# A selective scan inside a decoder: row-tiled 0/1 broadcasts of B and C, the gate's sigmoid on ScalarE, the gated output behind the first scan, and twelve inverse roots moved to the attention before

## What is computed

```python
z = h @ in_w.T                         # h: (16, 128, 256) after an RMS norm, z: 64 channels
gate = jax.nn.silu(h @ gate_w.T)
A = -jnp.exp(A_log)                    # 64 channels x 16 states
Bi, Ci = z @ Bp_w.T, z @ Cp_w.T        # 16 states for each row
dt = jax.nn.softplus(z @ dt_w.T + dt_b)
A_bar = 1.0 + dt[..., None] * A
state = a_bar * state + dtz_t[:, :, None] * b_t[:, None, :]    # one step in time
y = jnp.sum(state * c_t[:, None, :], axis=-1)
out = (y * gate) @ out_w.T
```

## Time and profile before

| | |
|---|---|
| median of three runs | 2480.36 us (2477.17 to 2481.49) |
| the profiled execution's own time | 2478.89 us |
| its span | 2477.2 us |
| PE busy | 2197.7 us (89%) |
| DVE busy | 1678.8 us (68%) |
| ACT busy | 1319.8 us (53%) |
| POOL busy | 808.0 us (33%) |

### The profile page before, as it was taken

How to read it: one execution, slowest core, us unless ns; L and a number is a source line. 1 busy time by engine, 2 the same in 40 slices (tenths; PEclk the granted TensorE clock), 3 DMA queues, 4 the chain that set the end, 5 groups by cost and what they waited for, 6 DMA issues and landing times. The chain is left out here.

```text
span 2477.2 us, 49397 instructions
## 1 busy us (share of the span) xinstructions
PE 2197.7 (89%) x17742; PEld 1801.8 (73%) x17744; DVE 1678.8 (68%) x3260; ACT 1319.8 (53%) x3083; POOL 808.0 (33%) x1022
## 2 busy tenths in 40 slices
PE   6979799999698797989999989999689897999774
PEld 5857587888476696778888568888568686888652
DVE  4767644774676596764677647666578785888858
ACT  4558635665487563542666343333487464545345
POOL 5656502333255442100233202222210100454365
PEclk9999979999899899979999999999799999999888
DMA  3000082113400000051211430000200003777710
GB/s 114 2 1 2 1 340 84 52 52 125 154 2 2 22 2 1 2 203 70 105 52 51 173 118 1 1 2 1 103 1 1 1 1 96 226 212 217 223 29 34
DMA packets 102936, 178.41 MB, mean 72 GB/s; under 512 B 59687, under 2 KB 71591, under 8 KB 97578
## 3 DMA queue, kind: packets, MB, share of 16 engines
q1 hardware_dynamic: 85514, 135.93, 16.5%
q0 software_dynamic: 9792, 28.85, 3.6%
q10 hardware_dynamic: 7392, 10.49, 1.2%
HBM read 112.44 MB, written 62.78 MB: 71 GB/s over the span
## 5 line engine op out<-in xcount | busy, mean ns | idle before, releaser
L2365 POOL TENSOR_TENSOR l2a_Pn<-l2a_Pn,l2a_rden 128x1024 f32<-128x1024 f32 x32 | 60.0, 1897 | 284.1 <-DVE l2a_rden L2604 284.1
L1631 ACT ACTIVATE l0f_w_parts<-l0f_W 128x512 fp32r (+1 forms) x117 | 90.4, 775 | 64.8 <-PE l0f_psG L1436 50.4
L1789 DVE TENSOR_TENSOR l0f_w_parts<-l0f_W,l0f_w_parts 128x512 fp32r<-128x512 f32 (+1 forms) x117 | 99.3, 867 | 37.5 <-ACT l0f_w_parts L1631 37.4
L1631 ACT ACTIVATE l1f_w_parts<-l1f_W 128x512 fp32r (+1 forms) x117 | 90.6, 775 | 62.9 <-PE l1f_psG L1436 50.2
L4197 POOL TENSOR_TENSOR l3x_Pn<-l3x_Pn,l3x_fac 128x616 f32<-128x616 f32 (+2 forms) x96 | 70.4, 761 | 150.4 <-DVE l3x_fac L4276 140.6
L1789 DVE TENSOR_TENSOR l1f_w_parts<-l1f_W,l1f_w_parts 128x512 fp32r<-128x512 f32 (+1 forms) x117 | 99.4, 867 | 12.4 <-ACT l1f_w_parts L1631 12.0
L1489 PE MATMUL l1f_psY<-l1f_W,l1f_XT_hT 128*128 (+1 forms) x440 | 104.2, 380 | 0.8 <-ACT l1f_XT_hT L1611 0.8
L884 ACT ACTIVATE l1a_att_Pn<-l1a_att_psS,l1a_att_nmx 128x128 f32<-128x128 f32 x256 | 92.1, 423 | 1.2 <-DVE l1a_att_nmx L1003 1.2
L884 ACT ACTIVATE l0x_Pn<-l0x_psS,l0x_nmx 128x128 f32<-128x128 f32 x256 | 92.1, 423 | 0.9 <-DVE l0x_nmx L1003 0.9
L1489 PEld LDWEIGHTS l1f_psY<-l1f_W,l1f_XT_hT 128*128 128x128 f32 x440 | 80.4, 190 | 10.8 <-issue 1.0
L707 POOL TENSOR_TENSOR l1a_att_Pn<-l1a_att_Pn,l1a_att_rden 128x512 f32<-128x512 f32 x64 | 66.5, 1039 | 64.8 <-DVE l1a_att_rden L1010 64.8
(11 more groups left out here) (883 smaller groups left out, 7603.8 us busy)
## 6 DMA issues: line engine op xcount, KB each, us to landing
relative_rows<-l3x_ext SPq DMA_DIRECT2D x32, 516.0 KB, 5.7
l1f_W<-in_l1f_w SPq DMA_DIRECT2D x9, 1536.0 KB, 21.7
l0f_W<-in_l0f_w SPq DMA_DIRECT2D x8, 1536.0 KB, 26.0
cumulative_rows<-l3x_cum SPq DMA_DIRECT2D x32, 384.0 KB, 3.3
l3x_K<-keys SPq DMA_DIRECT2D x16, 512.0 KB, 5.4
l3x_rel<-relative_rows SPq DMA_DIRECT2D x32, 231.0 KB, 4.3
values<-l1f_W SPq DMA_DIRECT2D x11, 512.0 KB, 5.3
l3x_V<-values SPq DMA_DIRECT2D x16, 308.0 KB
```

The lines of the kernel that those rows point to most:

```text
L1631: nc.scalar.activation(w_high[i], W[:, bass.ds(act_offsets[k] + o, m)], ACT.Copy).then_inc(high_ready, 1)
L1789: nc.vector.tensor_tensor(w_low[i], W[:, bass.ds(dve_offsets[k] + o, m)], w_high[i], ALU.subtract).then_inc(low_ready, 1)
L2365: nc.gpsimd.tensor_tensor(part, part, rden[b % 2][:, 8 * u:8 * u + 8].unsqueeze(2).to_broadcast([P, 8, P]), ALU.mult)\
```

## The change

B and C are first made compact: two full matmuls give 4 copies of 2 x 16 states in 128 rows (`states_by_row`, into psX), and ACT copies them to SBUF (`bc`). `to_channels` then spreads them with matmuls of 32 rows each whose stationary side, `pick`, holds zeros and ones and is made once by POOL; all 16 states are spread in one go, so B waits for both products of the pair before. The sigmoid is exp(-Ln(1 + exp(-gate))) on ACT in place of a reciprocal on DVE. `gate_y` stands between the two scans. The inverse roots of batches 0 to 11 (HEAD = 12) are made at the end of the attention, with a wait for its last use of the roots; the scan makes those of the last four, behind the normalising of its first two pairs. Cut to its core:

```diff
 softmax_attention, ACT, at the end
         if layer:
             early_roots(nc, G, act, mv_ready, head_ready)
+        else:
+            act.wait_ge(ms_ready, 2)
+            nc.scalar.activation(rt[:, 0:HEAD], ms[:, 0:HEAD], ACT.Sqrt, bias=eps[:, 0:1]).then_inc(root_ready, 1)
 softmax_attention, DVE, after add_y(i - 2), before moments(i - 3)
+            if not layer and i == NB:
+                dve.wait_ge(mv_ready, HEAD)
+                step.do(nc.vector.tensor_tensor(ms[:, 0:HEAD], means(G)[:, 0:HEAD], means(G)[:, 0:HEAD], ALU.mult))
+                nc.vector.tensor_tensor(ms[:, 0:HEAD], ms[:, 0:HEAD], variances(G)[:, 0:HEAD], ALU.add).then_inc(ms_ready, 1)
+            if not layer and i == NB + 1:
+                dve.wait_ge(root_ready, 2)
+                dve.wait_ge(xn_ready, NB)
+                nc.vector.reciprocal(G.rrms[:, 0:HEAD], rt[:, 0:HEAD]).then_inc(inverse_ready, 1)
 scan_loads: "B" and "C", [P, ST * P] each, become "BC", [P, 2 * P]
 selective_scan, POOL, at the start
+        step.do(nc.gpsimd.memset(pick[:, :], 0.0))
+        pick4 = pick[:, :].rearrange("p (q i c) -> p q i c", q=ST // 4, i=2)
+        for r in range(4):
+            step.do(nc.gpsimd.affine_select(out=pick4, in_=pick4, compare_op=ALU.not_equal, fill=1.0, base=-(32 + ST // 4) * r,
+                                            pattern=[[-1, ST // 4], [-ST, 2], [0, SC]], channel_multiplier=1))
+        nc.gpsimd.memset(G.pad[:, 7:8], 0.0).then_inc(picks_ready, 1)
 selective_scan, PE
-        pe.wait_ge(loaded, NL)
         def transpose_x(p):
             past(pe, hT_ready, p)
+            past(pe, bc_ready, p)
-        def inputs(p, h):
-            past(pe, weighted, 2 * (p - 1) + h + 1 if p else 0)
-            for s in range(h * HS, (h + 1) * HS):
-                ins = nc.tensor.matmul(psB[:, s * P:(s + 1) * P], bdB[:, s * P:(s + 1) * P], zg[p % 2][:, 0:P], start=True, stop=True)
-        def outputs(p, h): the same with bdC, behind u_ready
+        def states_by_row(p):
+            pe.wait_ge(z_ready, p + 1)
+            pe.wait_ge(hT_ready, p + 1)
+            for k in range(2):
+                ins = nc.tensor.matmul(psX[:, k * P:(k + 1) * P], bcw[:, k * P:(k + 1) * P], zg[p % 2][:, 0:P], start=True, stop=True)
+            ins.then_inc(bc_done, 1)
+        def to_channels(p, k):
+            for q in range(ST // 4):
+                for r in range(4):
+                    rows, s = slice(32 * r, 32 * r + 32), ST // 4 * r + q
+                    ins = nc.tensor.matmul(psB[:, s * P:(s + 1) * P], pick[rows, q * P:(q + 1) * P], bc[p % 2][rows, k * P:(k + 1) * P],
+                                           start=True, stop=True)
+            return ins
+        def inputs(p):
+            pe.wait_ge(bc_ready, p + 1)
+            past(pe, weighted, 2 * p)
+            to_channels(p, 0).then_inc(b_done, 1)
+        def outputs(p):
+            pe.wait_ge(u_ready, 2 * p + 2)
+            to_channels(p, 1).then_inc(c_done, 1)
 the loop on PE: inputs(p); sum_states(p - 1); project(p + 1); outputs(p); step_sizes(p + 1); states_by_row(p + 1); project_out(p - 1)
 selective_scan, ACT: the root and exp(A_log) move behind normalise(0) and normalise(1); in the loop
-            nc.scalar.activation(og[:, :], eg[:, :], ACT.Identity, bias=1.0).then_inc(gate_exp, 1)
+            act.wait_ge(bc_done, p + 1)
+            past(act, c_done, p - 1)
+            nc.scalar.activation(bc[p % 2][:, :], psX[:, 0:2 * P], ACT.Copy).then_inc(bc_ready, 1)
             (exp and Ln of the softplus)
+            nc.scalar.activation(og[:, :], eg[:, :], ACT.Ln, bias=1.0).then_inc(gate_exp, 1)
             (normalise(p + 2), which for batch HEAD waits for the late roots; A_bar's first half)
+            nc.scalar.activation(rg[p % 2][:, :], og[:, :], ACT.Exp, scale=-1.0).then_inc(rg_ready, 1)
 selective_scan, DVE: ms, rt and rrms for batches HEAD to 15 alone; gates(p) is gone; in the loop
             drive(p, 1)
+            scan(p, 0)
             if p:
                 gate_y(p - 1)
-            scan(p, 0)
             scan(p, 1)
-                gates(p + 1)
 more_layout, on the host: l1s_B and l1s_C become
+    A["l1s_BC"] = np.concatenate([states(I[f"L1_attn_{n}p_w"].T) for n in "BC"], axis=1)
+def states(w):
+    out = np.zeros((P, 4, 2, ST), w.dtype)
+    for i in range(2):
+        out[i * SC:(i + 1) * SC, :, i, :] = w[:, None, :]
+    return out.reshape(P, P)
```

More of the change, by code:

```diff
@@ L2001, in selective_scan @@
     L = G.ready.pop("scan")
-    inw, gatew, dtw, dtb, outw, alog, nw, bdB, bdC = (L.t[n] for n in ("in", "gate", "dtw", "dtb", "out", "Alog", "norm", "B", "C"))
+    inw, gatew, dtw, dtb, outw, alog, nw, bcw = (L.t[n] for n in ("in", "gate", "dtw", "dtb", "out", "Alog", "norm", "BC"))
     loaded, NL = L.loaded, L.count()
@@ L2015, in selective_scan @@
     ones = R.sb("ones", [P, P - 1])
+    bc = [R.sb(f"bc{i}", [P, 2 * P]) for i in range(2)]
+    pick = R.sb("pick", [P, ST // 4 * P])
     st6 = R.sb("st6", [P, 6 * NB])
@@ L2026, in selective_scan @@
         "b_done", "u_ready", "c_done", "scanned", "weighted", "sum_done", "yT_ready", "y_done", "x_ready"))
+    picks_ready, bc_done, bc_ready = (R.sem(n) for n in ("picks_ready", "inputs_outputs_done", "inputs_outputs_ready"))
     dt_ready, dtz_ready, rg_ready, gate_ready, abar_act, abar_pool, summed = (R.sem(n) for n in (
@@ L2120, in _ @@
         transpose_x(0)
+        pe.wait_ge(loaded, NL)
         project(0)
         step_sizes(0)
+        states_by_row(0)
+        pe.wait_ge(picks_ready, 1)
         for p in range(NP2):
@@ L2131, in _ @@
                 project(p + 1)
-            outputs(p, 0)
+            outputs(p)
             if p + 1 < NP2:
                 step_sizes(p + 1)
-            outputs(p, 1)
+                states_by_row(p + 1)
             if p:
@@ L2142, in _ @@
     def _(act):
[L2143 to L2147, removed]
         def normalise(p):
@@ L2157, in _ @@
         normalise(1)
+        act.wait_ge(ms_ready, 1)
+        nc.scalar.activation(rt[:, :], ms[:, :], ACT.Sqrt, bias=eps[:, 0:1]).then_inc(root_ready, 1)
+        act.wait_ge(loaded, NL)
+        nc.scalar.activation(alog[:, :], alog[:, :], ACT.Exp).then_inc(aexp_ready, 1)
         for p in range(NP2):
@@ L2181, in _ @@
             nc.scalar.activation(lv[:, :], ev[:, :], ACT.Ln, bias=1.0).then_inc(log_ready, 1)
+            act.wait_ge(gate_exp, 2 * p + 1)
+            past(act, rg_ready, p)
+            nc.scalar.activation(og[:, :], eg[:, :], ACT.Ln, bias=1.0).then_inc(gate_exp, 1)
             if p + 2 < NP2:
+                if 2 * (p + 2) == HEAD:
+                    act.wait_ge(rrms_ready, 1)
                 normalise(p + 2)
@@ L2197, in _ @@
         step.sig(nc.vector.memset(eps[:, :], RMS_EPS))
-        step.do(nc.vector.tensor_tensor(ms[:, :], means(G), means(G), ALU.mult))
-        nc.vector.tensor_tensor(ms[:, :], ms[:, :], variances(G), ALU.add).then_inc(ms_ready, 1)
+        step.do(nc.vector.tensor_tensor(ms[:, :], means(G)[:, HEAD:], means(G)[:, HEAD:], ALU.mult))
+        nc.vector.tensor_tensor(ms[:, :], ms[:, :], variances(G)[:, HEAD:], ALU.add).then_inc(ms_ready, 1)
         dve.wait_ge(root_ready, 1)
-        nc.vector.reciprocal(G.rrms[:, :], rt[:, :]).then_inc(rrms_ready, 1)
+        nc.vector.reciprocal(G.rrms[:, HEAD:], rt[:, :]).then_inc(rrms_ready, 1)
         dve.wait_ge(aexp_ready, 1)
         nc.vector.tensor_scalar(Am[:, :], alog[:, :], -1.0, None, ALU.mult).then_inc(am_ready, 1)
[L2205 to L2208, removed]
         def step_sizes(p):
@@ L4409, in used_inputs @@
     if "l1a" in t:
-        names |= {"l1s_" + n for n in ("in", "gate", "dtw", "dtb", "out", "Alog", "B", "C", "norm")}
+        names |= {"l1s_" + n for n in ("in", "gate", "dtw", "dtb", "out", "Alog", "BC", "norm")}
     if "l2x" in t:
```

28 lines of the change are left out of this document (9 added, 19 removed).

## The result

The changed kernel takes 2467.63 us (median of 17 runs) against 2480.36 of 17 of the kernel before: ratio 0.9946, 95% interval 0.9936 to 0.9955. It is faster by more than a measurement can blur, and the forecast was 2467.7. The profiled execution has an own time of 2466.35 and a span of 2464.6. As the steps will show, the sum came nearer than its terms did.

A forecast was written before the change was run, and what follows sets the result against it. PE bounds the loop at 13.43 us a pair, DVE 1.34 behind. Seven stretches gaining 1.63 each give 11.4, plus 1.0 at the head, less 0.5 for the clock: 11.9, so 2467.7 us, range 2462 to 2475.

The forecast's parts named there:

- The spread taken at 1.08: PE in the scan loop: B and C as 32-row matmuls take 1.08 us each, like the attention's scores.
- PE's need: PE's work per pair in the scan loop falls from 13.43 to 8.7 us, under DVE's need.
- 0.6 for meeting POOL: DVE's scans overlap POOL's work: 0.4 us lost on the first scan, 0.2 on the second, per pair.
- The collision's rule: DVE's scans and POOL's steps exclude each other: 0.7 us of overlap cost 0.7.
- The gating: DVE: moving it behind the first scan costs no time; the sum is awaited 2.2 us later, removing 1.34 idle.
- Ln's end: ACT's chain: Ln ends 10.7 us after dt's start T, DVE wants it at 11.2, so hidden by 0.5.
- The head: Scan's start: first hT 1.5 us earlier through early roots, 0.5 given back, so first dt 1.0 earlier.
- The first pair: First pair of the scan: no earlier pair to sum or add, so none of the loop's gain.
- The last sum: Last sum over states, at the scan's end: follows the same waits as before, so no change.
- The clock's rival: PE's clock falls behind its new gap in some pairs, each losing about 1 us; 2474 if all; 12 in 100.
- the forecast's allowance of 0.5: Taken off the summed gain: 0.5 us, half of one fall of PE's clock.
- The slower rival: PE's lower clock holds through the whole loop, seven stretches cost 33 us, about 2511; 5 in 100.

The follow-up runs named there:

- e2: The changed kernel with the gate's reciprocal back on DVE, ACT's Ln an Identity and its second Exp gone; 2473.07 us, ratio 0.9975.
- e3: The changed kernel with the gating of y ahead of the first scan, as before; 2478.06 us, ratio 0.9987.
- e12: The changed kernel itself, unaltered, measured again later on the same chip as other versions; 2465.79 us, ratio 0.9944.
- e6: The changed kernel with nine of the sixteen A_bar states on ACT and seven on POOL, in place of eight and eight; 2471.32 us, ratio 0.9955.
- e5: The changed kernel with all inverse roots made at the scan's start, as before; 2468.01 us, ratio 0.9935.
- e4: The kernel before with the 32-row broadcasts alone, and the PE and ACT orders that go with them; 2490.31 us, ratio 1.0042.
- e1: The changed kernel with B and C each spread by 16 full matmuls again, the rest of the change kept; 2490.62 us, ratio 1.0036.
- e11: The changed kernel with unread products in four places, nine A_bar states on ACT and step-size matmul ahead of C's spread from the second pair; 2460.28 us, ratio 0.9915.
- e7: The changed kernel with unread identity matmuls on PE at the scan's start, in the first pair, in the loop and ahead of the last sum; 2466.71 us, ratio 0.9928.
- e8: The changed kernel with unread identity matmuls in the loop alone, 5 a pair from the third pair on; 2469.47 us, ratio 0.9950.
- e9: The changed kernel with the gating ahead of the first scan and 7 unread identity matmuls a pair from the third on; 2478.81 us, ratio 0.9996.
- e10: The kernel before with the 32-row broadcasts alone and 7 unread identity matmuls a pair from the third on; 2479.96 us, ratio 1.0001.

## Why the prediction was right, and where its steps were not

**PE.** The spread taken at 1.08 is 1.10, changes of mode included. By an estimate, four row groups at once would take a quarter of today's 3.57, 0.89, so all else in a spread has some 0.2. The drain at a change of mode that the Trainium skill, "TensorEngine Tiling (Array Packing)", Key Properties, tells of is not seen by itself in these rows. PE's need was put at 8.7; it is busy for 9.31, still below DVE.

**DVE, the period.** 11.23 and 0.6 for meeting POOL were to make 11.8; it is 11.50. The term that was mis-sized is the 0.6: the first scan loses 0.28, the second next to nothing, because POOL's product, come later, waits for the first scan and its add for the second. (A scan alone takes 2.27, not the 2.23 of half of two records that overlap.) The collision's rule was seen, but its sign for the second scan depends on who starts first. The Trainium skill, "SBUF — State Buffer", SBUF: two separate sides, says so: whoever starts first keeps the shared port for the whole instruction, and VectorE takes part with two inputs from SBUF, against a GpSimd instruction that reads SBUF. The trace agrees: the scans and dtz, both of that kind, are held up (2.28 to 3.39, 0.29 to 1.96), u from psB beside POOL's steps is not (2.32). For the same reason the reciprocal, counted at 0.86, is worth 1.6 where the rest of the change stands (e2).

**The gating.** That the move costs no time and that the 1.34 of idle goes was right, and underrated. The step took the sum at its length at full clock; the new place gives it 2.5 us more (870.88 to 873.35). In the late pair of the changed kernel that was enough for a sum of 5.22, where e3 waits 2.04 to 2.16 in every pair; what that pair lost came by ACT's chain (0.57). Only in e12's longest pair was the sum late for the new place, by 0.84.

**ACT.** Ln's end was put at T + 10.7; it is T + 10.6 (e6 shows how near that is to being the bound). Hidden, as forecast.

**The head.** hT comes 1.85 earlier in place of 1.5, the first dt 1.34 in place of 1.0. By e5 the early roots give 1.80 of it, and the longer chain of B and C takes 0.46 back, forecast at 0.5 (e4 and e1 agree: 12.45 against 11.98, and 10.64 against 10.16). The attention's end, put at 0.2, costs 0.1: from its last add to the scan's first instruction on DVE are 2.56 us in place of 2.47.

**The first pair** is the step that failed: it was given "none of the loop's gain" and no loss, and it lost 2.10. PE has no sum there, is idle for 4.3 us ahead of `project`, and works at 1.2 GHz: the step-size matmul starts at 839.60 and dt waits 1.36 for ACT. e11, with PE at work in that time, has 11.49. But the clock needs ACT's longer chain to be felt: in e2, without the Exp and its table load ahead of hT, hT starts 3.20 behind dt in place of 4.83, and the first pair is 11.49 too, though C (2.09) and the step-size matmul (0.80) run at 1.2 GHz. **The last sum** was to change nothing and took 6.13 in place of 5.46; with PE at work ahead of it, it takes 3.84 (e7), so this is the clock.

**The clock's rival.** It had 12 in 100, "a pair with a fall loses about 1". It came in part: one stretch of the profile lost 0.64, two of e5 0.64 and 0.59, two of e12 0.65 and 0.68. In this profile the forecast's allowance of 0.5 was near what the loop lost; e12's 3.5, which a meeting on DVE began, was in no rival. The slower rival, half clock through the loop, did not come here, but its mechanism is real: e4 is slower by it than the kernel before. The Trainium skill, "TensorE: Matmul & The Clock Gate", HAM oscillation, tells of a loop whose every group of matmuls starts cold after a wait, there for loads: e3, waiting for DVE, does so in five pairs running, the changed kernel in some.

**The sum.** 11.9 was forecast, 11.19 found in that profile. Without the clock's share the loop gave 13.3 (10.83, 1.12, and 0.67 and 0.64 that the last sum and the late pair lost), 1.9 more than forecast, and the head 0.3 more; the clock, with ACT's chain behind it, took 2.10 + 0.67 + 0.64 = 3.4 where 0.5 was allowed. Two errors of opposite sign made the total right. That the median came within 0.1 us is luck besides: the two profiled executions differ by 12.54, of which 1.35 lie outside the scan's stage, and the changed kernel's runs spread from 2459.37 to 2475.16. (In the low end of the range, 7 x 2.23 + 1.6 is 17.2, not 17.0; this moves no bound by more than 0.2.)

What stays open: why the clock falls in one pair and not in the next of the same kernel was not tried beyond giving PE more work, and what lets POOL start ahead of dtz in two pairs was not tried at all.

## What to carry to other kernels

Before relieving an engine that is never idle, ask what its idleness will cost: PE freed of 4.1 us a pair lost its clock, and alone that made the kernel slower. A change can be worth 0.5% as a whole and nothing or less when one part is missing (e1 without the broadcasts, e3 without the gating's new place) or stands alone (e4), so undo each part from the whole as well as doing each alone. Give a consumer of PE room for the sum at half clock, or give PE something to do, and look whether the clock then holds: it did in the loops of e7, e8 and e11, not in those of e9 and e10.

## What was not expected of the hardware

Work whose results nobody reads can shorten a stage: 15 idle products ahead of the last sum took it from 6.13 to 3.84 us (e7), and e11, which has such products in four places, is the fastest version. The same pause can be followed by a fall of the clock or by none. Timeline of PE at the start of two pairs of e9:

```profile
883.41 1.17 PE L2125 MATMUL scan_psB<-scan_bc,scan_pick 32*128 32x128 f32 x32 [2.00 <-DVE scan_u L2282]
...
909.26 1.90 PE L2125 MATMUL scan_psB<-scan_bc,scan_pick 32*128 32x128 f32 x32 [2.00 <-DVE scan_u L2282]
```

B takes 1.17 behind the one pause of 2.00 and 1.90 behind the other, with the same work in the pair ahead of both (140 matmul records, 10.92 us). And a lead of 0.03 us in POOL's favour goes with 1.1 us more on DVE (e2, 872.82 against 872.85), one of 0.07 with 1.5 to 1.7 (e6, e12).
